# A vision tower block on one core: where VectorE makes the low parts of the experts' matrices around the last batch's second norm

## The reference

```python
h = ssm_convolution(x, ...)                      # (8, 256, 512): 8 batches of 256 tokens
h = concatenate([cls_tok, h], axis=1)            # one class row ahead of each batch: 257 rows
h = h + attention(layernorm(h), ...)             # 16 heads of 32
router_logits = einsum('bsh,he->bse', layernorm(h), router_w) + router_b
top 2 of 8 experts for every token, gates from their probabilities
expert_out = gelu(x @ expert_w[e] + expert_b[e])
h = h + (sum of gated expert_out) @ out_w + out_b
```

## Time and profile before

| | before |
|---|---|
| median of three runs | 748.42 us (747.17 to 749.06) |
| profiled execution, its own time | 749.32 us |
| its span | 747.6 us |
| busy: PE, DVE, ACT, POOL | 679.0, 526.1, 413.2, 151.3 us |
| mean granted clock of TensorE | 0.968 |

### The profile page before, as it was taken

The page is one execution under the profiler, slowest core; times in us unless marked ns, Lnnn a source line. Parts: engine busy times, 40 slices in busy tenths (PEclk is TensorE's granted clock), DMA queues, the critical chain, the costliest instruction groups (busy, mean ns, idle before and its releaser), DMA issues.

```text
span 747.6 us, 16676 instructions
## 1 busy us (share of the span) xinstructions
PE 679.0 (91%) x5671; PEld 543.2 (73%) x5672; DVE 526.1 (70%) x1211; ACT 413.2 (55%) x1071; POOL 151.3 (20%) x306
## 2 busy tenths in 40 slices
PE   4688887879999999999999999888769999998998
PEld 4477877867778787777878777656448888886786
DVE  7988993556778777787877876678774444445775
ACT  4865544476667677676766766575623333333111
POOL 5200001010121111202112120113032333326560
PEclk9899999989999999999999999999779999999999
DMA  7500356400000010000100004125716765656894
GB/s 208 189 2 15 128 114 147 97 1 1 3 21 37 0 53 3 28 28 14 42 0 28 28 28 145 54 74 208 254 56 195 205 203 169 168 166 203 258 324 175
DMA packets 54553, 76.11 MB, mean 102 GB/s; under 512 B 24666, under 2 KB 26970, under 8 KB 54387
## 3 DMA queue, kind: packets, MB, share of 16 engines
q1 hardware_dynamic: 40850, 42.43, 17.6%
q0 software_dynamic: 5920, 19.40, 9.9%
q10 hardware_dynamic: 7744, 13.77, 5.0%
HBM read 45.42 MB, written 30.16 MB: 101 GB/s over the span
## 4 chain that ended last, share of the span: by engine, by line
PE 74%; DVE 13%; ACT 6%; DMA 3%; issue 2%; POOL 1%; ACTq 0%; DVEq 0%; POOLq 0%
PE ps L1969 45%; PE ps L2072 9%; PE ps L2082 4%; PE ps L2065 4%; PE ps L2133 4%; DVE ring L1401 3%; DVE ring L1402 3%; PE ps L1916 2%; DMA wo_raw<-in_L_attn_Wo_dram 2%; PE ps L2089 1%; ACT prb L1021 1%; DVE ew_lo L1713 1%; ACT pts L1029 1%; PE ps L2032 1%; PE ps L1960 1%
## 5 line engine op out<-in xcount | busy, mean ns | idle before, releaser
L1029 ACT ACTIVATE pts<-ps 128x512 f32<-128x512 f32 x128 | 77.1, 602 | 97.5 <-PE ps L2072 97.4
L1021 ACT ACTIVATE prb<-ps,negmax 128x257 f32<-128x257 f32 x256 | 117.7, 478 | 4.7 <-DVE negmax L1472 3.7
L1472 DVE TENSOR_REDUCE negmax<-ps 128x2 f32<-128x514 f32 x128 | 82.5, 686 | 21.4 <-PE ps L2065 21.4
L2072 PE MATMUL ps<-ident,prb 128*128 128x128 f32 x512 | 83.9, 288 | 6.2 <-ACT pts L1029 3.2
L2072 PEld LDWEIGHTS ps<-ident,prb 128*128 128x128 f32 x512 | 57.3, 144 | 30.7 <-issue 12.0
L1481 DVE TENSOR_SCALAR prb<-prb,rrec 128x258 f32<-128x258 f32 x256 | 73.4, 351 | 2.3
L1203 ACT ACTIVATE rows<-ps 128x512 f32<-128x512 f32 x40 | 23.9, 598 | 84.7 <-DVE ps L1826 82.7
L1969 PE MATMUL ps<-ew_hi,xnT_hi 128*128 x160 | 67.0, 419 | 0.1
L1969 PE MATMUL ps<-ew_lo,xnT_hi 128*128 x160 | 63.4, 396 | 0.0
L1969 PE MATMUL ps<-ew_hi,xnT_lo 128*128 x160 | 63.1, 394 | 0.0
L1746 DVE TENSOR_TENSOR xnT_lo<-ps,xnT_hi 128x512 fp32r<-128x512 f32 x40 | 27.7, 691 | 49.6 <-ACT xnT_hi L1163 31.1
(11 more groups left out here) (402 smaller groups left out, 1772.5 us busy)
## 6 DMA issues: line engine op xcount, KB each, us to landing
y_slots<-rows ACTq DMA_DIRECT2D x40, 256.0 KB
ew<-in_L_ffn_expert_w_dram SPq DMA_DIRECT2D x8, 1024.0 KB, 9.0
h_dram<-h_ob SPq DMA_DIRECT2D x17, 256.0 KB, 2.0
xn_dram<-tok SPq DMA_DIRECT2D x17, 256.0 KB, 2.2
h_late<-h_dram SPq DMA_DIRECT2D x12, 256.0 KB
out_dram<-h_late SPq DMA_DIRECT2D x11, 256.0 KB
y_slots<-u_sb SPq DMA_DIRECT2D x9, 256.0 KB, 5.8
tok_dram<-so SPq DMA_DIRECT2D x4, 512.0 KB, 3.2
```

The costliest lines, as they stand in the source:

```text
L1021: e = act.activation(prb[:, u % 2, j, 0:KEYS], ps[:, j, 0:KEYS], ACT.Exp, bias=negmax[:, u % 2, j:j + 1], accum_out=rowsum[:, u % 2, j:j + 1])
L1029: act.activation(pts[:, slot:slot + 2, :, st * P:(st + 1) * P], ps[:, 4, :].rearrange("p (h t s) -> p h t s", h=2, t=HALVES), ACT.Copy).th ...
L1472: dve.tensor_reduce(negmax[:, u % 2, 2 * b:2 * b + 2], ps[:, 2 * b:2 * b + 2, 0:KEYS], AX_X, ALU.max, negate=True).then_inc(s["dve_max"], 1)
L2072: mm = pe.transpose(ps[:, 4, (2 * j + tt) * P:(2 * j + tt + 1) * P], prb[:, u % 2, 2 * b + j, tt * P:(tt + 1) * P], ident[:, :])
```

## The change

Three things are moved; no work is added or left out, but one low part is cut into two instructions.

- **VectorE at the last batch.** The low parts of experts 0 and 1 stood ahead of the last batch's first add, and that of expert 2 between its two adds. Now only `top_two(1)` stands ahead. The first half of expert 0's low part is between the adds, its second half behind the statistics, and then `normalise` for both tiles, which stood behind the class tile's statistics. Expert 1's low part takes their place there, ahead of the class tile's norm. Expert 2's is made behind the gates.
- **ScalarE.** The last head group's high part (`hi_ot(last, 3)`) goes ahead of expert 0's. Experts 2 and 3 are made one place later.
- **VectorE at the table.** The reading of the slots' tokens (`token_of`) goes ahead of seven small instructions that make `slot_of`, `expert_of` and `stores_used`.

```diff
@@ ScalarE, behind the last batch's attention
             act.wait_ge(s["pe_values"], NB * HALVES)
+            hi_ot(last, 3)
             hi_expert(0)
-            hi_ot(last, 3)
             hi_expert(1)
             act.wait_ge(s["pe_pv"], NB * KC)
-            hi_expert(2)
...
                 if q == EARLY_QUADS:
-                    hi_expert(3)
+                    hi_expert(2)
                 keep_lgT(q)
+            hi_expert(3)
             hi_expert(4)
@@ VectorE, behind the last batch's attention
+            def lo_chunks(e, k0, k1):
+                dve.wait_ge(s["act_expert_high"], e + 1)
+                return dve.tensor_tensor(ew_lo[:, e, k0:k1, :], ew[:, e, k0:k1, :], ew_hi[:, e, k0:k1, :].bitcast(F32),
+                                         ALU.subtract)
+
             def lo_expert(e, done=1):
-                dve.wait_ge(s["act_expert_high"], e + 1)
-                dve.tensor_tensor(ew_lo[:, e, :, :], ew[:, e, :, :], ew_hi[:, e, :, :].bitcast(F32), ALU.subtract
-                                  ).then_inc(s["dve_expert_low"], done)
+                lo_chunks(e, 0, KC).then_inc(s["dve_expert_low"], done)
 
             top_two(1)
-            for e in range(2):
-                lo_expert(e)
             residual(last, 0, 6)
             dve.wait_ge(s["dve_residual"], last * HALVES + 1)
             residual_stats(last, 0)
-            lo_expert(2)
+            lo_chunks(0, 0, KC // 2)
             residual(last, 1, 7)
             dve.wait_ge(s["dve_residual"], last * HALVES + 2)
             residual_stats(last, 1)
             dve.wait_ge(s["dve_stats2"], 5 * last + 2)
             norm_sums(last)
+            lo_chunks(0, KC // 2, KC).then_inc(s["dve_expert_low"], 1)
+            for st in range(HALVES):
+                normalise(last, st)
             dve.wait_ge(s["loaded_cls"], 16)
             dve.wait_ge(s["pe_cls_projected"], 1)
...
-            for st in range(HALVES):
-                normalise(last, st)
+            lo_expert(1)
             dve.wait_ge(s["pool_rstd"], NB + 1)
             dve.wait_ge(s["pool_out_bias"], NT)
@@ VectorE, the table of slots
                 dve.tensor_tensor(of_place[:, c0:c1, :], bc(iota_p[:, :].unsqueeze(1), shape),
                                   bc(slot_place[:, c0:c1].unsqueeze(2), shape), ALU.is_equal).then_inc(s["dve_onehot"], 1)
+            dve.wait_ge(s["pe_token_of"], 1)
+            then(dve.tensor_copy(token_tile[:, :], ps[:, 2, 0:SLOTS]))
+            dve.scalar_tensor_tensor(out=token_of[:, :], in0=token_tile[:, :], scalar=float(P),
+                                     in1=ps[:, 2, SLOTS:2 * SLOTS], op0=ALU.mult, op1=ALU.add
+                                     ).then_inc(s["dve_token_of"], 1)
+
             then(dve.tensor_scalar(slot_of[:, :], slotf[:, :], -1.0, None, ALU.add))
...
             dve.tensor_scalar(stores_used[:, :], pairs_used[:, 1:2], 16.0, None, ALU.mult).then_inc(s["dve_stores_used"], 1)
-            dve.wait_ge(s["pe_token_of"], 1)
-            then(dve.tensor_copy(token_tile[:, :], ps[:, 2, 0:SLOTS]))
-            dve.scalar_tensor_tensor(out=token_of[:, :], in0=token_tile[:, :], scalar=float(P),
-                                     in1=ps[:, 2, SLOTS:2 * SLOTS], op0=ALU.mult, op1=ALU.add
-                                     ).then_inc(s["dve_token_of"], 1)
-
             dve.wait_ge(s["act_route_exp"], 1)
...
-            e = LOWS_IN_ATTENTION + 1
-            dve.tensor_tensor(ew_lo[:, e, 2:KC, :], ew[:, e, 2:KC, :], ew_hi[:, e, 2:KC, :].bitcast(F32), ALU.subtract)
-            dve.wait_ge(s["act_expert_high"], e + 2)
-            dve.tensor_tensor(ew_lo[:, e + 1, :, :], ew[:, e + 1, :, :], ew_hi[:, e + 1, :, :].bitcast(F32), ALU.subtract)
+            lo_expert(2)
+            lo_chunks(LOWS_IN_ATTENTION + 1, KC // 2, KC)
+            lo_chunks(LOWS_IN_ATTENTION + 2, 0, KC)
```

## The result

| | before | after |
|---|---|---|
| median | 747.64 us (742.52 to 751.34, 21 runs) | 743.42 us (739.27 to 748.20, 21 runs) |
| after by before | | 0.9948, 95% interval 0.9930 to 0.9966 |
| profiled execution, its own time | 749.32 us | 743.4 us |
| its span | 747.6 us | 741.6 us |
| mean granted clock of TensorE | 0.968 | 0.970 |

A forecast was written before the change was run, and what follows sets the result against it. TensorE was taken as the bound, except from 505 to 555 us, where the chain turns to VectorE. Gains 3.9 + 0.4 − 0.2 = 4.1 us took the profiled 749.32 to 745.2, the median to 744.3; range 742.0 to 746.7.

The forecast's parts named there:

- The adds and the norms: Last batch on VectorE: first add at 507.8 us instead of 512.4, both tiles normed at 515.7, before TensorE wants them.
- The wait for L1508: TensorE's 2.42 us wait at 520.75 for the last batch's norm, forecast to vanish with the clock staying up.
- Rival (d): Last batch's tiles not normed before TensorE wants them; 2.3 us of room, total near 744.5; chance within the forecast's 0.57.
- The class tile is late next, behind expert 1's low part: That low part holds GpSimd's class power until 520.4; class norm at 522.3, TensorE idle 1.8 us before turning the tile.
- rival (a): GpSimd's class power gets in ahead of expert 1's low part or isn't held: gain 6.1, median 742.3 us; chance 0.24.
- I take 2.0 since the new idle time may cost the clock again: Class tile's turning to VectorE's logits: 2.0 us, against 2.32 before and 1.65 at full clock; logits at 524.4.
- Gain 0.4: Earlier table reading: gathers start 0.8 us earlier, but low parts then bound the slots, matmuls at 554.3 instead of 554.73.
- I take 0.2, nearer zero: Loss at the first slot tile from TensorE's lower clock after idling 2.2 us right ahead of the slots.
- the bound of 1.1: Most the clock could lose at the first slot tile: recovery later by the 2.2 us idle, at half the price.
- rival (c): TensorE's clock stays down for more slot tiles, 1.9 us each; kernel slower, near 751 us; chance 0.04.
- The gathers: GpSimd coming second waits for VectorE's low part; second gather at 547.4, just ahead of low parts at 547.8, stays hidden.
- rival (b): Gathers caught behind low parts ahead of the slots: held for all three, gain 0.8, 747.6 us; for one, no loss; chance 0.15.

## Why the prediction was right

The forecast for the median was 744.3 us in a range of 742.0 to 746.7; 743.42 was measured. The gain by the second slot tile is 4.13 where 4.1 was forecast, and the change's own rows bear most steps out. Two terms were mis-sized, by 0.8 and by 0.7 us, and they cancel: that the sum is right to 0.03 is luck. Of the 0.9 us between forecast and median 0.8 is the kernel before itself, whose median was 748.42 in three runs and 747.64 beside the changed kernel.

- **The adds and the norms: right.** Forecasts put on the same count: the first add at 4.54 (measured 4.47), the last batch's power done at 11.39 (11.29), both tiles normed at 12.44 (12.40). The wait for L1508 is gone and the clock stays at 1.00 until 520. Rival (d) fell.
- **The class tile is late next, behind expert 1's low part: right**, and rival (a) with it. Idle time ahead of it 1.89 where 1.8 was forecast, and the run with that low part elsewhere shows the cause (power 0.69 for 2.66, wait gone). GpSimd lost by 0.17 us. That is close, but it isn't chance: VectorE's next instruction stood 0.17 ahead of the power in the kernel before too (520.14 and 520.31), and 0.17 to 0.18 ahead in all nine executions in which one with two SBUF inputs follows the class statistics at once. These two starts would have priced rival (a) lower than 0.24. (With the norm there, in the two runs that put the norms back, the power came first.)
- **"I take 2.0 since the new idle time may cost the clock again": mis-sized.** From the class tile's turning to the logits it took 1.56, all of it at the upper level; the clock fell only behind it. With the class tile turned 0.33 earlier than forecast (expert 1's low part began 0.19 earlier, and the power ended 0.55 behind it, not 0.70), that makes 4.71 instead of 3.9.
- **"Gain 0.4" for the table: right in size (0.31), and the reason too.** The copy comes 0.69 earlier behind the logits (0.8 forecast), the first slot tile waits for `xnT_lo` and for no gather, and half a low part taken away moved it by as much. But the table's part is worth 4.12 alone by the second slot tile and 2.94 by the ninth, and behind the last batch's part it costs 0.80 by the second and gains 0.35 by the ninth. A sum that prices it once, with everything in, can't tell this, and the prediction's text shows nothing of it.
- **"I take 0.2, nearer zero" for the clock at the experts: mis-sized.** The slots' first tile took 5.48 instead of 4.68, and from first to second slot 0.89 was lost, near the bound of 1.1. The reason given for nearer zero was that TensorE had stood waiting there before, too. In this execution TensorE idles 2.53 us right ahead and runs all twelve matmuls at 0.50, where before the last four were back at the upper level. The fillers show what hangs on it: 2.55 us. But the 0.89 isn't the change's for certain: of the seven other runs in which TensorE idled right ahead of the first slot tile (0.89 to 4.57 us) and had no fillers between the turnings and the tile, six took 4.59 to 4.89 us to the second slot, about as much as the kernel before, and one 5.70. The idle time alone doesn't decide it, and what does stays open. This is the mechanism of rival (c), but the next slot tile already took 2.77: far from what would have turned the sign.
- **The gathers: the reading was right, the page's inferred sentence didn't hold.** Gathers issued under a low part took 1.1 to 3.0 us and ended 0.80 to 0.85 behind the one that ran at their issue; those issued under small steps took 0.96 to 1.39, also where a low part began 0.2 us behind their issue (541.12 and 541.34 in the changed kernel). The Trainium skill, page SBUF — State Buffer, section Who interferes with whom, infers that `tensor_tensor` leaves descriptor generation alone; here the gathers issued in the middle of one waited. Whether it is the read of the index or the writing of descriptors that waits, no run tells. Each was held to the end of one instruction only, though low parts followed back to back, so rival (b) "held for all three" was priced too high: caught, the second gather took 1.77 instead of 0.96 where the last batch alone was changed. In the changed kernel it was issued 0.22 ahead of the low parts, where 0.4 was forecast.

That the earlier norms matter through the clock more than through the wait itself wasn't in the prediction: undoing them alone returned 3.5 us of the 4.71, with the class norm only 0.6 later, and with fillers in the waits the stretch behind them shrank from 4.5 to 2.4 us.

What stays open: the worth of ScalarE's new order, what decides how long the clock stays low in the first slot tile, and by how much the total time follows a gain of under 1 us at a slot tile, since medians of one kernel moved by as much from one comparison to the next (before: 747.07 to 748.05).

## What to carry to other kernels

Price an idle time of a bound TensorE twice, once as idle time and once as the clock of what comes next: here, behind waits of 0.8 to 2.5 us, the next matmuls cost up to twice as much in some places and nothing more in others, and matmuls that nobody reads got it back, as long as they end before the real work is ready. A VectorE instruction with two SBUF inputs and a GpSimd instruction or gather take turns, one instruction each, so put such a VectorE instruction where GpSimd is in the middle of nothing that others wait for, and keep short steps as cover while gathers are issued. Measure two parts of a change apart and together, and count a few tiles past the place where they meet: two that gain 4.1 and 4.9 us alone by the second slot tile gained 4.1 together, and by the ninth 2.9 and 4.1 alone and 4.5 together, since behind either part the slots wait next for VectorE's low parts, or for a gather held behind one. Less VectorE work ahead of the slots, a class norm that no longer waits for GpSimd's bias add and a TensorE kept at its upper clock gained 4.7 more.

## What the runs showed of the hardware that I had not expected

- GpSimd's tiny power (128x2) took 0.69 us undisturbed and 1.06, 1.60 and 2.66 under VectorE instructions with two SBUF inputs, always ending some 0.55 behind them. Begun 0.17 behind a norm, which has one, it took 0.92 (the kernel before).
- It works the other way round too: a half low part begun at 507.18 under GpSimd's bias add took 1.81 instead of 1.21, and a norm (`tensor_scalar`, one SBUF input, 128x512) took 1.85 instead of 0.55 beside one.
- The granted clock fell behind two waits of 0.79 and 1.10 us (norms put back) so that the next sums took 1.72. Behind one wait of 1.89 (changed kernel) they took 0.96, at the upper level, behind one of 2.07 (ScalarE's order undone) 1.20. The length of the last wait alone doesn't tell whether the clock falls, nor, at the first slot tile (4.59 to 5.76 us behind waits of 2.4 to 2.5), how long it stays low.
